# Two adapter layers on one core: tiles 8 to 31 in pairs by Strassen's seven block products, and layer 0 added to turned x in PSUM

## What is computed

```python
# layer 0: each request has its own rank-16 adapter out of 64
Bx  = einsum('bni,bri->bnr', x, L0_B[id0]);  x1 = x + einsum('bnr,bor->bno', Bx, L0_A[id0])
# layer 1: dense W, and a gated mixture of 8 rank-16 adapters
logits = x1 @ Wr.T + 5 * one_hot(lang)
gates  = softmax of the two largest logits, at their two experts
h      = einsum('btd,erd->bter', x1, A)
out    = x1 + x1 @ W.T + 2 * einsum('bter,bte,eor->bto', h, gates, B)
```

## Time and profile before

| | us |
|---|---|
| median of 3 runs | 523.01 (520.01 to 524.23) |
| span of the profiled execution | 523.2 |
| PE busy | 510.4 (98%) |
| DVE busy | 383.9 (73%) |
| ACT busy | 240.6 (46%) |
| POOL busy | 171.1 (33%) |

### The profile page before, as it was taken

The page is one execution under the profiler, slowest core; times in us unless marked ns, Lnnn a source line. Parts: engine busy times, 40 slices in busy tenths (PEclk is TensorE's granted clock), DMA queues, the critical chain, the costliest instruction groups (busy, mean ns, idle before and its releaser), DMA issues.

```text
span 523.2 us, 9432 instructions
## 1 busy us (share of the span) xinstructions
PE 510.4 (98%) x3350; PEld 465.7 (89%) x3350; DVE 383.9 (73%) x882; ACT 240.6 (46%) x543; POOL 171.1 (33%) x159
## 2 busy tenths in 40 slices
PE   7699999999899999999999999999999999999997
PEld 6588999889899899999989899998989999898997
DVE  5779686758879686977968697796969779693441
ACT  4655433545354544445454445554544545543221
POOL 5442325634314434142443414143441414321000
PEclk9799999999999999999999999999999999999999
DMA  8942455637757768477785857878576767633301
GB/s 330 322 114 82 130 134 170 205 111 233 231 185 231 229 153 260 169 219 238 245 239 152 248 184 222 247 222 245 155 225 207 243 225 213 202 105 98 122 40 41
DMA packets 52467, 99.76 MB, mean 191 GB/s; under 512 B 6716, under 2 KB 35260, under 8 KB 52420
## 3 DMA queue, kind: packets, MB, share of 16 engines
q1 hardware_dynamic: 45744, 78.14, 48.7%
q0 software_dynamic: 6656, 20.98, 12.7%
q10 hardware_dynamic: 20, 0.03, 0.0%
HBM read 69.24 MB, written 29.88 MB: 189 GB/s over the span
## 4 chain that ended last, share of the span: by engine, by line
PE 87%; DVE 7%; issue 2%; ACT 1%; DMA 1%; POOL 1%; another core or an unknown queue 0%; DVEq 0%; POOLq 0%
PE o_bank L609 69%; PE o_bank L622 8%; PE b_bank L501 2%; PE o_bank L598 2%; PE x_bank L529 2%; DMA a_in<-in_L_cond_A_dram,a_run 1%; DVE a_raw L945 1%; PE x_bank L519 1%; DVE x_lo L882 1%; PE b_bank L486 1%; DVE xt L917 1%; PE x_bank L486 1%; ACT bx_pair L758 1%; DVE w_in L924 0%; DVE b_raw L935 0%
## 5 line engine op out<-in xcount | busy, mean ns | idle before, releaser
L609 PE MATMUL o_bank<-w_hi,x_hi 128*128 128x512 f32 (+1 forms) x744 | 255.6, 344 | 0.0
L609 PE MATMUL o_bank<-w_lo,x_hi 128*128 128x512 f32 (+1 forms) x744 | 251.1, 337 | 0.0
L609 PE MATMUL o_bank<-w_hi,x_lo 128*128 128x512 f32 (+1 forms) x744 | 250.9, 337 | 0.0
L417 POOL TENSOR_TENSOR a_t<-a_raw,a_t 64x1024 fp32r<-64x1024 f32 x30 | 72.3, 2411 | 248.9 <-ACT a_t L731 178.3
L609 PEld LDWEIGHTS o_bank<-w_hi,x_hi 128*128 128x128 f32 x744 | 139.8, 188 | 13.5 <-issue 3.2
L609 PEld LDWEIGHTS o_bank<-w_lo,x_hi 128*128 128x128 f32 x744 | 139.9, 188 | 10.1
L609 PEld LDWEIGHTS o_bank<-w_hi,x_lo 128*128 128x128 f32 x744 | 139.7, 188 | 10.2
L945 DVE STREAM_TRANSPOSE a_raw<-a_in 128x1024 f32<-128x1024 f32 x32 | 65.3, 2044 | 2.8 <-DMA a_in<-in_L_cond_A_dram,a_run 2.8
L388 POOL DMA_INDIRECT a_in<-in_L_cond_A_dram,a_run x64 | 61.0, 952 | 19.3 <-issue 19.0
L731 ACT CAST a_t<-a_raw 128x1024 fp32r<-128x1024 f32 x32 | 33.6, 1050 | 70.0 <-DVE a_raw L945 69.9
L805 ACT COPY out_sb<-o_bank 128x376 f32<-128x376 f32 (+2 forms) x96 | 39.5, 443 | 52.6 <-PE o_bank L622 52.6
(11 more groups left out here) (111 smaller groups left out, 504.3 us busy)
## 6 DMA issues: line engine op xcount, KB each, us to landing
out_dram<-out_sb SPq DMA_DIRECT2D x31, 512.0 KB
x_in<-in_x_dram SPq DMA_DIRECT2D x120, 128.0 KB
w_in<-in_x_dram SPq DMA_DIRECT2D x25, 512.0 KB
x_dram<-w_in SPq DMA_DIRECT2D x25, 512.0 KB, 4.4
w_in<-x_dram SPq DMA_DIRECT2D x100, 128.0 KB
w_in<-in_L_cond_W_dram SPq DMA_DIRECT2D x6, 512.0 KB, 13.3
x_in<-in_x_dram SPq DMA_DIRECT2D x2, 512.0 KB
out_sb<-in_L_cond_W_dram SPq DMA_DIRECT2D x2, 512.0 KB, 15.1
```

What stands on the lines that cost most here:

```text
L417: nc.gpsimd.tensor_tensor(lower, a_raw[Q:P, m % 2, :], lower.bitcast(F32), ALU.subtract)\
L609: mm = pe.matmul(O[part][:, 0:hi - lo], xs[:, n % 2, c, :], w[:, c, lo:hi], start=(k == 0), stop=(k == K3 - 1), skip_group_check=True)
```

## The change

K is now 8, and tiles 8 to 31 are taken in 12 pairs (a, b). Part 0 (512 columns) is computed for each tile as before (`pair_first_part`). The other 648 columns of W are two blocks of H = 324. With x1 of the pair as a 2 by 2 block matrix (a or b; features 0 to 511 or 512 to 1023), the four output blocks come from seven products of 12 matmuls of 324 columns (`product`, L737) in place of eight. Three of them use sums of W's blocks, T1 to T3, which POOL makes in fp32 during tiles 3 to 6 (`t_chunk`, ten tensor operations for each of four chunks), and ACT and DVE split; T4 takes the place of one block of w. Four use sums of x1 blocks, S1 to S4: `make_s` on DVE makes three and `make_s4` on POOL one, ACT makes their high halves and POOL the low ones (`s_lo`). Partial results go from bank to bank by ACT (`copy_ab`, `copy_bc`, `copy_cd`, `copy_s7`), and two output blocks end with a DVE addition (`out_b1`, `out_b2`).

x1 of tiles 7 to 31 no longer goes through DRAM. DVE turns x (`turn_x`) straight into `xt`; ACT copies `xt` into the two banks SX (`put_part`), `add_l0` adds its eight matmuls there, and ACT and DVE split the sum (`raw_hi`, `raw_lo`), ACT keeping three of four halves in fp32 too (`keep_raw`, into `xt`). Both tiles of a pair use the same two banks, one after the other. The loads of x rows, the stores and the loads of `x1_dram` and DVE's turn of it fall away.

PE's list for a pair, cut by its waits on banks:

```diff
-            for n in range(1, T):
+            for n in range(1, K):
...
+            for q in range(PAIRS):
+                a, b = K + 2 * q, K + 2 * q + 1
+                more = b + 2 < T
+                pair_first_part(q, 0)
...
+                product(a1_slot(q), *w_block(0, 0), PA, True)
...
+                wait_sum(q, S3)
+                product(s3_slot(q), *t_block(2), PD, True)
+                if more:
+                    make_bx(a + 2)
+                pe.wait_ge(ab_copied, q + 1)
+                wait_sum(q, S2)
+                product(s2_slot(q), *t_block(1), PB, False)
+                turn_gated(a, bx_count(a + 2) + 1 if more else bx_count(T))
+                product(A2, *w_block(1, 0), PA, False)
+                pe.wait_ge(gt_ready, 2 * (a + 1))
+                pair_lora(a, 0, O[0])
+                pair_lora(a, 1, PA)
+                if more:
+                    make_bx(b + 2)
+                    add_l0(a + 2)
+                pair_first_part(q, 1)
+                pe.wait_ge(bc_copied, q + 1)
+                wait_sum(q, S1)
...
+                product(s1_slot(q), *t_block(0), PC, False)
+                product(B2, *w_block(0, 1), PB, False)
+                if more:
+                    add_l0(b + 2)
+                turn_gated(b, bx_count(b + 2) + 1 if more else bx_count(T))
+                pe.wait_ge(cd_copied, q + 1)
+                wait_sum(q, S4)
+                product(s4_slot(q), *w_block(1, 1), PC, False)
+                pe.wait_ge(gt_ready, 2 * (b + 1))
+                pair_lora(b, 0, O[0])
+                pair_lora(b, 1, PB)
+                pair_lora(b, 2, PD)
+                pair_lora(a, 2, PC)
```

ACT's list for a pair:

```diff
+            for q in range(PAIRS):
...
+                if more:
+                    put_part(a + 2)
+                    a_hi_part(a + 2)
+                exp_part(a)
+                copy_ab(q)
+                s1_hi(q)
+                copy_s7(q)
+                s4_hi(q)
...
+                if more:
+                    swap_part(a + 2, a + 3)
+                    pair_part(a + 2)
+                copy_bc(q)
+                pair_out(a, 0, O[0], LA0, z_out)
+                pair_out(a, 1, PA, LA1, c11_out)
+                if more:
+                    swap_part(b + 2, b + 3)
+                    pair_part(b + 2)
+                    split_a(a + 2)
+                    put_part(b + 2)
+                    a_hi_part(b + 2)
+                exp_part(b)
+                copy_cd(q)
+                if more:
+                    split_b(b + 2)
+                    s3_hi(q + 1)
+                    s2_hi(q + 1)
+                pair_out(b, 0, O[0], LB0, z_out)
+                pair_out(a, 2, PC, LA2, c12_out)
```

A product on PE, the block sums of W on POOL, and the splits and sums of x1:

```diff
+            def product(slot, hi_at, lo_at, bank_out, start):
+
+                for k in range(3 * CB):
+                    c = k // 3
+                    low, w = ((0, hi_at), (0, lo_at), (1, hi_at))[k % 3]
+                    mm = pe.matmul(bank_out[:, 0:H], xs[:, slot, low, c, :], w[:, c, :],
+                                   start=(start and k == 0), stop=(k == 3 * CB - 1), skip_group_check=True)
+                mm.then_inc(p_psum, 1)
...
+                step(t1, hi[:, top_c, w2], hi[:, top_c, w1], ALU.subtract, 0)
+                step(t4, lo[:, top_c, w2], lo[:, top_c, w1], ALU.subtract, 0)
+                step(t1, t1, t4, ALU.add, 2)
...
+            for m in range(3, K + 2):
+                a_lo_part(m, m + 1, m + 1)
+                pool.wait_ge(a_lo_ready, m + 1)
+                reload_b(m + 2)
+                reload_a(m + 2)
+                if 4 <= m < 4 + CB:
...
+                    t_chunk(m - 4)
...
+            def s_lo(q, which, slot, raw):
+                pool.wait_ge(ss_hi, 4 * q + which)
+                nc.gpsimd.tensor_tensor(xs[:, slot, 1, :, :], raw, xs[:, slot, 0, :, :].bitcast(F32),
+                                        ALU.subtract).then_inc(ss_lo, 1)
...
+            def a_lo_paired(m, last_b, last_a):
+                pool.wait_ge(a_hi_ready, m + 1)
...
+            for q in range(PAIRS):
...
+                    a_lo_paired(a + 2, a + 3, a + 3)
+                s_lo(q, S1, s1_slot(q), xt[:, 1, chunks(0), :])
+                s_lo(q, S4, s4_slot(q), xt[:, 1, chunks(1), :])
...
+                    a_lo_paired(a + 3, min(a + 5, T - 1), min(a + 4, T - 1))
...
+            def put_part(m):
...
+                        act.wait_ge(sh_ready, HB * j)
+                        act.wait_ge(sl_ready, HB * j)
...
+                if j % 2 == 0 or h == 0:
+                    dve.wait_ge(t_copied, 3 * (j // 2) + (h if j % 2 == 0 else 2) + 1)
+                slot = raw_slot(j, h)
+                minus(xs[:, slot, 1, :, :], bank_chunks(SX[h]), xs[:, slot, 0, :, :]).then_inc(sl_ready, 1)
...
+            def make_s(q, which):
+
+                b = K + 2 * q + 1
+                dve.wait_ge(t_copied, 3 * q + 3)
...
+                a1, b1, b2 = xt[:, 0, chunks(0), :], xt[:, 1, chunks(0), :], xt[:, 1, chunks(1), :]
+                x1, x2 = bank_chunks(SX[0]), bank_chunks(SX[1])
+                dst, src, other, op = ((a1, a1, x1, ALU.subtract), (b1, b1, x2, ALU.add),
+                                       (b2, x2, a1, ALU.subtract))[which - 1]
+                nc.vector.tensor_tensor(dst, src, other, op).then_inc(s_step, 1)
...
+            def sums_of_pair(q):
+                b = K + 2 * q + 1
+                make_s(q, 1)
+                raw_lo(b, 0)
+                make_s(q, 2)
+                make_s(q, 3)
+                raw_lo(b, 1)
```

More of the change, by code:

```diff
@@ L68, in sem, with over @@
             return ctx.enter_context(nc.semaphore(name))
+        def over(*tensors):
+            with ExitStack() as ended:
+                return [ended.enter_context(nc.sbuf_tensor(name, shape, dt)) for name, shape, dt in tensors]
         w_hi = sb("w_hi", [P, SHIFT + C * PITCH], F32R)[:, SHIFT:].rearrange("p (c w) -> p c w", c=C)
@@ L623, in add_lora, with pair_lora, pair_first_part @@
                                    start=False, stop=(k == 2), skip_group_check=True)
-                mm.then_inc(o_psum, 1)
+                return mm
+            def add_lora(n, part):
+                lora_products(n, part, O[part]).then_inc(o_psum, 1)
+            def pair_lora(n, part, bank_out):
+                lora_products(n, part, bank_out).then_inc(so_psum, 1)
+            def pair_first_part(q, side):
+                j = 2 * q + side
+                if q == 0 and side == 0:
+                    pe.wait_ge(out_ready[0], K)
+                else:
+                    pe.wait_ge(z_out, j)
+                pe.wait_ge(sh_ready, HB * (j + 1))
+                lo, hi = PARTS[0]
+                for k in range(K3):
+                    c = k // 3
+                    if k % (3 * CB) == 0:
+                        pe.wait_ge(sl_ready, HB * j + c // CB + 1)
+                    low, w = ((0, w_hi), (0, w_lo), (1, w_hi))[k % 3]
+                    mm = pe.matmul(O[0][:, 0:hi - lo], xs[:, raw_slot(j, c // CB), low, c % CB, :], w[:, c, lo:hi],
+                                   start=(k == 0), stop=(k == K3 - 1), skip_group_check=True)
+                mm.then_inc(h_psum, 1)
@@ new lines, in t_split, with t_last_split, t1_hi @@
+            def t_split(c):
+                act.wait_ge(t_step, 10 * c + 10)
+                for k in range(1, 3):
+                    nc.scalar.copy(t_w[:, k, 0, c, 0:H], t_raw[:, k, 1, c, 0:H]).then_inc(t_hi, 1)
+            def t_last_split(c):
+                nc.scalar.copy(w_hi[:, c, col_half(1)], t_raw[:, 0, 0, c, 0:H]).then_inc(f_hi, 1)
+            def t1_hi(c):
+                act.wait_ge(f_lo4, c + 1)
+                nc.scalar.copy(t_w[:, 0, 0, c, 0:H], t_raw[:, 0, 1, c, 0:H]).then_inc(f_hi, 1)
@@ L853, in _ @@
                     xt_part(3)
-                if n == K - 4:
-                    a_hi_part(n + 2)
-                if n % 2 == 0 and n >= K - 1:
-                    for m in a_tiles(n):
-                        a_hi_part(m)
+                if n == K - 1:
+                    a_hi_part(K + 1)
                 exp_part(n)
@@ new lines, in _ @@
+                if K - CB <= n < K:
+                    t_split(n - (K - CB))
+                out_part(n, 2)
+            s3_hi(0)
+            s2_hi(0)
+            for q in range(PAIRS):
+                a, b = K + 2 * q, K + 2 * q + 1
+                more = b + 2 < T
+                if q == 0:
+                    act.wait_ge(o_psum, NP * K)
+                    for c in range(CB):
+                        t_last_split(c)
+                if more:
[6 more added lines that the diff above has]
+                s4_hi(q)
+                if q == 0:
+                    for c in range(CB):
+                        t1_hi(c)
+                if more:
[18 more added lines that the diff above has]
+                pair_out(a, 2, PC, LA2, c12_out)
@@ L1173, in _ @@
-                if not turn_again:
-                    gated_t_part(n)
```

(13 more changed lines are left out.)

623 lines of the change are left out of this document (394 added, 229 removed).

## The result

The changed kernel takes **609.88 us** (median of 4 runs, 601.89 to 615.70) against 523.55 before on the same chip: slower, by 86 us. The ratio, 1.156 (95% interval 1.148 to 1.164), is that of the two faster runs, with mean granted clocks of 0.969 and 0.980, while the profiled execution is one of the two slower, with 0.944.

The account below looks back on a forecast made before the run. PE was taken to bound the kernel before; 523.2 + 4 (making T) + 1.1 (layer 0) + 4.4 (pair 0) + 59.4 (pairs 0 to 10) - 1.5 (last pair) gave 591 us, range 555 to 615.

Parts of the forecast that it names:

- ahead of tile 8: Start-up: making T in tiles 3 to 6 costs 4 us, layer 0 of tiles 7 to 9 costs 1.1.
- the walk: Step-by-step timing of one pair through the engines' ordered lists: PE's waits lengthen it from 30.40 to 35.8 us.
- the dense pair: A pair in which PE never waits: 29.4 us, 1.0 less than before.
- First wait: At a's low-rank products and make_bx(b + 2): PE waits 1.2 and 1.4 us for DVE's gated columns and turn of x.
- Second wait: At add_l0(b + 2): PE waits 2.1 us for the adapter's turn, high half and POOL's low half.
- Third wait: Toward the next pair's part 0: b's gating held by POOL, 0.4 us; ACT's late copy of O[0], 1.3 us.
- The low halves of 128 x 512: POOL's low-half steps in a pair: 1.2 us each by elements, not in the way of DVE's held gating steps.
- My rival of 511 us: Over the pairs: all waits hide, PE reaches 29.4 us a pair, 511 us in all; chance 4%.
- The clock falls: In the pairs: one fall of PE's clock a pair, 3 us lost, about 625 us; chance 5%.
- The rival on T's preparation: T's making in tiles 3 to 6 delays more, or gathers come late in the pairs: 600 to 615 us; chance 14%.
- my own case: Whole kernel, with the waits as walked: 575 to 600 us, chance 63%.
- Half of the waits hidden: In the pairs: handoffs or a chain are shorter, 30.4 + 2.2 us a pair, about 555 us; chance 12%.

Follow-up runs that it names:

- e4: Changed kernel with the edits of e1 and e2, turn_x(b + 2) split in halves around the gated columns, and O[0]'s copy ahead of S2's high half: 551.73 us.
- e5: e4 with POOL's order turned, the low halves of S1 and S4 ahead of the low half of a + 2's adapter: 536.84 us.
- e1: Changed kernel with the weighing of the experts in five DVE operations, none reading two SBUF tensors, in place of eight: 590.81 us.
- e2: Changed kernel with DVE's turn of b + 2's adapter ahead of x1's low halves, and ACT's high half of it ahead of put_part: 604.77 us.
- e3: Changed kernel without making or splitting T1 to T4; their products read blocks of w instead, so compute something else: 591.27 us.
- e6: e5 without the sums of W's blocks, left out as in e3: 523.66 us.

## Why the prediction was right

The direction and the range held: 591 predicted, 555 to 615 given, 609.88 measured. It lies near the upper end of the range, and every part came out above its prediction. The parts, against the profiled 611.1:

| | predicted, us more than before | measured |
|---|---|---|
| ahead of tile 8 | 5.1 | 10.5 |
| pair 0 | 9.8 (4.4 + 5.4) | 12.0 |
| pairs 1 to 10, waits | 54 | 56 |
| pairs 5 to 10, clock | 0 | 9 |
| last pair and end | -1.5 | 0.0 |

- **A steady pair** was 35.8 by the walk and is 35.97. PE busy was to be 82% and is 86%; DVE 26 us of 36 and is 28.5, since held steps count as busy. The agreement of the sum is better than that of its terms, and so in part luck: the dense pair was 0.6 us too short and the waits, 6.4 by the walk, are 6.0.
- **First wait** (1.2 at the low-rank products, 1.4 at `make_bx(b + 2)`): 1.06 and 0.95. Right in place. That the order makes it is supported by e4 and e5, in which the turn of x goes ahead and both waits are gone; e4 has the edits of e1 and e2 in it as well, but neither of these alone takes the two waits away.
- **Second wait** (2.1 at `add_l0(b + 2)`): 1.30, and 1.6 us of a pair go with it (e2). In e1, where PE comes earlier, it is 1.6 on the mean (13.1 in 8).
- **Third wait.** This is the step that failed in its cause. I held the gating of b for 0.4 us and wrote "Two of its small steps read two SBUF tensors"; it is the gating of a that waits, 1.19 us, and I said of POOL's low halves of S that they "are not in its way". They are: behind `a_t`'s step POOL makes S1's and S4's low halves at 328.17, and the two steps on eight columns end with them. By e1 this is worth up to 1.4 us a pair. The copy of O[0] costs 0.47, not 1.3.
- **The low halves of 128 x 512**, "by elements ... 1.2 us", take 1.3 (1.27 each at 328.17), against 2.39 for 64 x 1024. The 324-column steps take 0.88, near the upper of my two estimates, and tiles 3 to 6 with their tail cost 12.5 us (e3) where I took 4 from 0 to 10: outside its own bounds, and the term that was mis-sized most. Part of it is the clock, which I had put at full there. I counted DVE's held steps but let tile slack cover them; those on the way to the gated columns and to `bx_t` have none.
- **The dense pair**, 29.4, is 30.0 (e5). The 84 matmuls save 1.5 in place of 1.8, since those behind a turn or another kind of product start about 0.08 late; `add_l0` gives 0.87 back in place of 0.76; and `make_bx` twice for one tile costs 0.2 more than once for two. My rival of 511 us was thus out of reach even with every wait hidden: e6, with no sums too, takes 523.66.
- **Rivals.** "The clock falls", 5%, came true in half of the pairs of the profiled execution, at half of its price (1.5 us a pair in place of 3), since a fall replaces the wait at L610. The rival on T's preparation, 600 to 615, had its price there: 7.6 us more than my own case ahead of and in pair 0. Neither alone reaches 611; the two (7.6 and 9), the last pair (1.5) and the steady pairs (2) make the 20 us between. The 9 us of the clock hold for this execution: outside pairs 5 to 10 it spent 27 us at half clock, which alone gives a mean of about 0.98, and since a mean of 0.980 was measured too (601.89 us), I estimate that these falls need not come. Half of the waits hidden is e4, 551.73, but only after the orders were rewritten.

What stays open: why the clock falls in one pair and not in its twin, and how often it does so from one execution to the next. It falls at the end of a row of three waits (L571, L704, L586, 3.2 us of waits within 5.3); the changed kernel's pairs 1 to 4 have the same three at the same distances and keep the full clock. How the losses ahead of tile 8 and in pair 0 divide between waits and clock is not shown either.
